# Decoder layer on one core: the loads, the out-projection and the late softmax around the change of phase, put in another order

## The chip, the cores and the metric

One core of a Trainium2 chip. The time is the device time of one execution in microseconds (us). The kernel before ran three times: 1143.99, 1139.13 and 1143.78 us, median 1143.78.

## The reference

x and a context are 16 sequences of 256 rows of 512 values (4096 rows), float32.

```python
x = layernorm(x + attn(x) @ Wo.T + bo)      # per row: 32x32 scores over heads, softmax, a difference of two halves, RMS norm
r = scan(r * decay + ctx * ctx)             # along each sequence
x = layernorm(x + x * r)
h = relu(x @ w1.T) ** 2                     # 2048 wide, w1 and w2 ternary by groups of 64
x = layernorm(x + rmsnorm(h) @ w2.T)
```

The attention here mixes the 16 heads of one row with each other; it is small and private to the row, and takes many small matmuls, with a softmax on VectorE. Each float32 operand of a large matmul is split into an upper and a lower part.

## The kernel before

The 4096 rows are eight superblocks of 512 (`NSB` 8, four tiles of 128 rows each, `TT` 4). Every engine has its own program in order, tied to the others by semaphores, and the order is written out by hand.

**Phase A** (`phase_a`, bodies 0 to 7): body i projects superblock i to q, k and v (`project`, 12 groups of 12 matmuls, line 615), does the scores of i-1 (`scores`, four chunks of 64 matmuls, line 632) with their softmax, and the mix with v of i-2 (`mix`, line 651). Beside it the weights of the feed-forward part are made ternary in `w_in`: loaded on the SP queue (line 473 and 469), taken by ScalarE (line 941), worked on by GpSimd, and written back.

**The transition** stands after `phase_a` in each engine's program: scores of superblock 7 (`LATE`), the four `mix` chunks of superblock 6, and what superblock 0 needs before its feed-forward: `out_project` (line 740, 48 matmuls), `add_projection` (line 1330), `scan` of the squared context (line 1363), `x1_norm`, `add_scan` (line 1372), `x2_norm`, and the transposes of the result (`x2_transpose` line 774, `x2_upper` line 996 on ScalarE, `x2_lower` line 1390 on VectorE). `mixed_turn` (line 1242) on VectorE empties a mix bank and lets the next `mix` start; `out_lower` (line 1325) makes the lower half of the operand that `out_project` reads. SP issues the loads one by one: `dbd`, `ot` (line 522), the second half of q (line 402), `woh`, `wol`, `bob`, `xb`, `cx` (lines 543 to 547), then weights.

**Phase B** (`phase_b`, bodies 0 to 7): body i is the feed-forward of superblock i in 16 steps j: `up` (line 788), `hidden` on ScalarE (lines 1005 to 1015), `hidden_lower` (line 1398) and `hidden_sum` (line 1409) on VectorE, `down` (line 804) three steps behind. In the same steps stand the last norm of i-1 (`hidden_rms` line 1421, `add_hidden` line 1430) and all the preparation of i+1. So `out_project(i + 1, t)` stands at j = 2 to 5, and from t = 1 on waits for `add_projection(i + 1, t - 1)`; `x2_transpose(i + 1, ...)` stands at the end of the body. GpSimd adds the bias to `xb` (`add_bias`, line 1595, four instructions a body); in `body_b(i)` it adds that of i+1 and before the change waits for nothing but the load of `xb`. Superblock 7's softmax is fitted into bodies 0 to 2 of phase B: `late_clean`, `late_shift` (line 1188 to 1192), the exponential on ScalarE (line 928) and `late_second` (line 1201 to 1217), at steps that the tables `LATE_CLEAN`, `LATE_SHIFT`, `LATE_EXP` and `LATE_SECOND` give; its RMS scale (`o_scale`, line 1567) is GpSimd's in body 4.

The memory of a region is reused: `xb`, `cx` and `x2n` lie where the halves of the transposed x lay in phase A.

Of the kernel before, what the change touches and what calls it, by code (L numbers as in the profile page):

```python
# [29 lines left out]
P = 128  # L30
# [44 lines left out]
def program(nc, x_in, xt_in, ctx_in, w_qkvo, bo, lq1, lq2, lk1, lk2, decay, fc_in, proj_in, out):  # L75
# [11 lines left out]
    with ExitStack() as stack:  # L87
# [95 lines left out]
        vo = sb("x", "vo", [P, HD, G], F32)  # L183
        xb = sb("x", "xb", [P, TT, D], F32)
        bob = sb("x", "bob", [P, D], F32)
        cx = sb("x", "cx", [P, KC, SB], F32)
        x2n = sb("x", "x2n", [P, TT, D], F32)
        x2h = sb("x", "x2h", [P, KC, SB], F32R)
        x2l = sb("x", "x2l", [P, KC, SB], F32R)
# [170 lines left out]
        LATE_CLEAN = {1: 1, 4: 2, 11: 3}  # L360
        LATE_SHIFT = {1: 1, 4: 2, 13: 3}
        LATE_EXP = {1: 0, 2: 1, 6: 2, 14: 3}
        LATE_SECOND = {1: (0, 2), 2: (1, 3)}
        LATE_MIX = {(2, 11): 0, (3, 1): 1, (3, 4): 2, (4, 1): 3}
# [14 lines left out]
        def _(sp):  # L379
# [81 lines left out]
            def x_load(i, par):  # L461
                hold((f_ps, at(i - 1, 12, 0)) if later(i - 1) else (xa_ld, 16))
                sp.dma_start(x_raw[:, par, :, :], xt_in[i]).then_inc(xa_ld, 16)

            def w_load(i, u):

                if u:
                    hold((wt_wr, at(i, 32, 16)))
                    sp.dma_start(w_in[:].rearrange("p (r d) -> p r d", d=D), proj_in[i]).then_inc(wt_ld, 16)
                    return  # L470
                if later(i):
                    hold((wt_wr, at(i, 32, 0)))
                sp.dma_start(w_in[:].rearrange("p (k n) -> p k n", k=KC), fc_in[i]).then_inc(wt_ld, 16)
# [23 lines left out]
            def body(i, par, do_2, do_1):  # L497
                if later(i) and not (isinstance(i, int) and i == NSB - 1):
                    x_load(i + 1, 1 - par)
# [24 lines left out]

            def cx_load(i):
                sp.dma_start(cx[:], ctx_in[i]).then_inc(cx_ld, 16)

            def w1_load(n):
# [12 lines left out]
            ot_load(0)  # L541
            second_half_load(NSB - 1)
            sp.dma_start(woh[:].bitcast(F32), wo_scr[0]).then_inc(wo_ld, 16)
            sp.dma_start(wol[:].bitcast(F32), wo_scr[1]).then_inc(wo_ld, 16)
            sp.dma_start(bob[:], bo.rearrange("(a n) -> a n", a=1).to_broadcast([P, D])).then_inc(bo_ld, 16)
            sp.dma_start(xb[:], x_t[0]).then_inc(xb_ld, 16)
            cx_load(0)

            w_write(NSB - 1, 1)
# [6 lines left out]
            w1_load(1)  # L556
            o_write(NSB - 2)
            w2_load(1)
            hold((rs_ps, TT))
            cx_load(1)  # L560
            hold((x2_done, TT))
            sp.dma_start(xb[:], x_t[1]).then_inc(xb_ld, 16)

            def body_b(i, prep, fin):
# [35 lines left out]
        def _(pe):  # L600
# [239 lines left out]
            mix(NSB - 2, 2, 0, G // 4)  # L840
            scores(NSB - 1, 2, 0, FULL)
            mix(NSB - 2, 3, 0, G // 4)
            for t in range(TT):
                out_project(0, t)
            scores(NSB - 1, 3, 0, FULL)
            for t in range(TT):
                scan_transpose(0, t)
            for t in range(TT):
                x2_transpose(0, t)
# [34 lines left out]
        def _(act):  # L884
# [141 lines left out]
            for t in range(1, LANES, 2):  # L1026
                act.dma_start(dbd[H * t:H * (t + 1), t, :, :],
                              dt[H * t:H * (t + 1), :, :]).then_inc(dbd_ld, 16)
            mixed(NSB - 2, 0)
            mixed(NSB - 2, 1)  # L1030
            out_upper(0)
            mixed(NSB - 2, 2)
            mixed(NSB - 2, 3)
            for k in range(KC):
                ctx_square(0, k)
            for t in range(TT):
                x2_upper(0, t)

            def body_b(i, prep, fin, ahead):
                for j in range(HC):  # L1040
# [15 lines left out]
                    if not later(i) and j == 0:  # L1056
                        out_upper(1)
                    if not later(i) and j in LATE_EXP:
                        exps(LATE, LATE_EXP[j])
                    if (i, j - 1) in LATE_MIX:  # L1060
# [23 lines left out]
        def _(v):  # L1084
# [356 lines left out]
            late_turn(0)  # L1441
            late_turn(1)
            mixed_turn(NSB - 2, 0)
            mixed_turn(NSB - 2, 1)
# [3 lines left out]
            out_lower(0)  # L1448
            late_turn(2)
            mixed_turn(NSB - 2, 3)  # L1450
            square_sum(NSB - 2, 2)
            square_sum(NSB - 2, 3)
            rms_seed(NSB - 2)
            add_projection(0, 0)
            add_projection(0, 1)
            v.wait_ge(dec_ld, 64)
            scan(0, range(2))
            add_projection(0, 2)
            scan(0, range(2, 4))
            add_projection(0, 3)  # L1460
            late_turn(3)
            x1_norm(0)
            for t in range(TT):
                add_scan(0, t)
            x2_norm(0)
            for t in range(TT):
                x2_lower(0, t)

            def body_b(i, prep, fin, ahead):
                if not later(i):  # L1470
                    late_clean(0)
                for c in LATE_SECOND.get(i, ()):
                    late_second(c)
                for j in range(HC):
# [33 lines left out]
                    if not later(i) and j in LATE_SHIFT:  # L1508
                        late_shift(LATE_SHIFT[j])
                    if (i, j) == (2, 0):  # L1510
                        late_diff_turn()
# [19 lines left out]
        def _(pool):  # L1531
# [70 lines left out]
            def body_b(i, prep, fin, ahead):  # L1602
                if prep:
                    for t in range(TT):
                        add_bias(i + 1, t)
# [49 lines left out]
```

## Time and profile before

| | |
|---|---|
| median of three executions | 1143.78 us |
| the profiled execution's own time | 1143.45 us |
| its span, first to last instruction | 1141.6 us |
| TensorE busy | 1047.9 us, 92% |
| VectorE, ScalarE, GpSimd busy | 928.6, 566.6, 245.2 us |
| mean granted TensorE clock | 0.963 |

The profile is of one execution; 1.85 us lie outside its span. In a row of the timeline the first number is the start in us from the span's start, the second the duration, and a bracket gives the idle time of that engine before the row and what ended it. PE is TensorE, DVE VectorE, ACT ScalarE, POOL GpSimd, SPq and ACTq are the DMA issues of SyncE and ScalarE. The granted clock is a share of 2.4 GHz; 0.50 is 1.2 GHz. Phase A ends near 451 us, the first `up` of body 0 starts at 519.5 us, and bodies 1 to 6 take 73.6 to 80.5 us each.

### The profile page before, as it was taken

What the parts mean: (1) busy time and instruction counts of PE and PEld (TensorE: products, weight loads), DVE (VectorE), ACT (ScalarE), POOL (GpSimd) and SP (SyncE); (2) the same over time, 40 slices, a digit from 0 to 9 for tenths busy, and PEclk for the clock granted to TensorE, in tenths of its full rate; (3) what the DMA queues carried; (4) which work ended last, traced back from release to release, by engine and by line L of the source; (5) the groups of instructions that cost most, each with busy time, mean ns of one, the idle gap of its engine ahead of it and who ended that gap; (6) DMA issues with size and microseconds to landing.
All of it is one profiled execution on the core that took longest, in us unless ns stands there. A gap on an engine that the chain in (4) does not pass through costs nothing.

```text
span 1141.6 us, 19562 instructions
## 1 busy us (share of the span) xinstructions
PE 1047.9 (92%) x7008; PEld 826.8 (72%) x7008; DVE 928.6 (81%) x1669; ACT 566.6 (50%) x866; POOL 245.2 (21%) x238
## 2 busy tenths in 40 slices
PE   7999999998999998727989999999999999999994
PEld 5777667676776766515867888878877788888883
DVE  4579898888888998596987998978969969798555
ACT  5442424243434342205556566665663766656672
POOL 6212433434252425131020020020023100200000
PEclk9999999999999999867998999999999999999997
DMA  7977686859596859892120223312202303110011
GB/s 277 306 183 177 144 238 129 247 133 240 134 246 137 213 144 210 239 358 83 38 74 1 74 75 61 112 44 50 106 1 74 111 2 88 61 38 1 1 37 37
DMA packets 167469, 140.50 MB, mean 123 GB/s; under 512 B 140368, under 2 KB 140880, under 8 KB 161488
## 3 DMA queue, kind: packets, MB, share of 16 engines
q1 hardware_dynamic: 96080, 113.83, 36.3%
q10 hardware_dynamic: 71296, 25.43, 9.1%
q8 instruction: 58, 0.95, 0.4%
q14 instruction: 35, 0.29, 0.1%
HBM read 82.61 MB, written 52.95 MB: 119 GB/s over the span
## 4 chain that ended last, share of the span: by engine, by line
PE 61%; DVE 17%; DMA 6%; ACT 6%; issue 5%; SPq 4%; ACTq 1%; DVEq 0%
PE ps_s L804 17%; PE ps_f L788 17%; PE ps_f L615 11%; PE ps_s L632 6%; PE ps_o L740 5%; SPq L432 2%; SPq L402 2%; DVE row_sum L1144 1%; DMA cx<-in_ctx_turned 1%; DMA w_in<-in_fc_turned 1%; DVE cx L1363 1%; DMA w_scr<-w_in 1%; DMA w_raw<-in_qkvo 1%; DMA qbd<-q_scr 1%; ACT f_sb L913 1%
## 5 line engine op out<-in xcount | busy, mean ns | idle before, releaser
L788 PE MATMUL ps_f<-x2h,w 128*128 128x512 f32 x512 | 205.4, 401 | 1.6 <-DVE x2l L1390 1.6
L788 PE MATMUL ps_f<-x2l,w 128*128 128x512 f32 x512 | 201.4, 393 | 0.0
L804 PE MATMUL ps_s<-w,hh 128*128 128x512 f32 x500 | 198.5, 397 | 2.8 <-DVE hl L1398 2.8
L804 PE MATMUL ps_s<-w,hl 128*128 128x512 f32 x500 | 196.5, 393 | 0.0
L615 PE MATMUL ps_f<-xth,wh 128*128 128x512 f32 x376 | 156.6, 416 | 3.4 <-issue 2.7
L1398 DVE TENSOR_TENSOR hl<-h_sb,hh 128x512 fp32r<-128x512 f32 x128 | 93.1, 727 | 81.7 <-ACT hh L1015 81.5
L615 PE MATMUL ps_f<-xtl,wh 128*128 128x512 f32 x376 | 147.8, 393 | 0.0
L615 PE MATMUL ps_f<-xth,wl 128*128 128x512 f32 x376 | 147.7, 393 | 0.0
L632 PE MATMUL ps_s<-qbd,k 128*32 128x128 f32 x2048 | 124.9, 411 | 15.3 <-DMA qbd<-q_scr 15.3
L1595 POOL TENSOR_TENSOR xb<-xb,bob 128x512 f32<-128x512 f32 x32 | 48.8, 1554 | 403.3 <-DMA xb<-in_x 403.3
L632 PEld LDWEIGHTS ps_s<-qbd,k 128*32 128x32 f32 x2048 | 83.0, 147 | 52.4 <-issue 12.8
L1005 ACT ACTIVATE r_sb<-ps_f 128x512 f32<-128x512 f32 x128 | 75.5, 590 | 87.3 <-PE ps_f L788 87.3
L1023 ACT ACTIVATE h_sq<-h_sb 128x512 f32<-128x512 f32 x128 | 79.4, 620 | 74.4 <-DVE h_acc L1409 74.4
L788 PEld LDWEIGHTS ps_f<-x2h,w 128*128 128x128 f32 x512 | 97.6, 191 | 22.2 <-issue 2.5
L788 PEld LDWEIGHTS ps_f<-x2l,w 128*128 128x128 f32 x512 | 97.5, 190 | 19.5
L804 PEld LDWEIGHTS ps_s<-w,hh 128*128 128x128 f32 x500 | 94.8, 190 | 22.6 <-issue 3.2
L804 PEld LDWEIGHTS ps_s<-w,hl 128*128 128x128 f32 x500 | 94.9, 190 | 19.3
L1576 POOL TENSOR_TENSOR w_in<-w_in,gscale 128x512 f32<-128x512 f32 x32 | 52.7, 1646 | 225.2 <-DVE gscale L1269 212.2
L615 PEld LDWEIGHTS ps_f<-xth,wh 128*128 128x128 f32 x376 | 71.7, 191 | 31.2 <-issue 15.5
L913 ACT ACTIVATE f_sb<-ps_f 128x512 f32<-128x512 f32 x64 | 38.4, 599 | 112.4 <-PE ps_f L615 108.9
L1409 DVE TENSOR_TENSOR h_acc<-h_acc,h_sq 128x512 f32<-128x512 f32 x112 | 84.2, 752 | 0.1
L1015 ACT ACTIVATE hh<-h_sb 128x512 fp32r<-128x512 f32 x128 | 81.0, 633 | 4.1
(160 smaller groups left out, 1830.7 us busy)
## 6 DMA issues: line engine op xcount, KB each, us to landing
q_scr<-f_sb ACTq DMA_DIRECT2D x32, 256.0 KB, 4.3
k_scr<-f_sb ACTq DMA_DIRECT2D x32, 256.0 KB, 2.7
w_scr<-w_in SPq DMA_DIRECT2D x16, 512.0 KB, 5.8
k<-k_scr SPq DMA_DIRECT2D x8, 1024.0 KB, 8.0
qbd<-q_scr SPq DMA_DIRECT2D x128, 64.0 KB, 4.7
v_scr<-f_sb ACTq DMA_DIRECT2D x32, 256.0 KB, 5.7
ot<-o_scr SPq DMA_DIRECT2D x32, 256.0 KB, 4.6
xb<-in_x SPq DMA_DIRECT2D x8, 1024.0 KB, 5.3
```

Of the source, the lines that this page charges most:

```text
L615: last = nc.tensor.matmul(ps_f[:, n % 2, :], w[:, n // 4, k, cols], xx[:, par, k, :], start=(k == 0 and xx is xth and w is wh), stop=(k == ...
L632: last = nc.tensor.matmul(ps_s[32 * j:32 * (j + 1), 2 * (c % 2) + gq // 4, (gq % 4) * P:(gq % 4 + 1) * P], k2[:, :, g], qbd[:, :, :, g].re ...
L740: last = nc.tensor.matmul(proj_bank(i, t), a[:, k, rows], w[:, k, :], start=(k == 0 and w is woh and a is oth), stop=(k == KC - 1 and a is ...
L788: last = nc.tensor.matmul(ps_f[:, j % 2, :], w1[:, j // 2, k, (j % 2) * P:(j % 2 + 1) * P], xx[:, k, :], start=(k == 0 and xx is x2h), sto ...
L804: last = nc.tensor.matmul(ps_s[:, t, :], a[:, j % 4, t * P:(t + 1) * P], w2[:, j, :], start=(j == 0 and a is hh), stop=(j == HC - 1 and a ...
L913: nc.scalar.activation(f_sb[:, n % 3, :], ps_f[:, n % 2, :], ACT.Copy).then_inc(f_ev, 1)
L1005: nc.scalar.activation(r_sb[:], ps_f[:, j % 2, :], ACT.Relu).then_inc(r_done, 1)
L1015: nc.scalar.activation(hh[:, j % 4, :], h_sb[:, j % 4, :], ACT.Copy).then_inc(hh_done, 1)
L1023: nc.scalar.activation(h_sq[:, j % 2, :], h_sb[:, j % 4, :], ACT.Square).then_inc(hq_done, 1)
L1398: nc.vector.tensor_tensor(hl[:, j % 4, :], h_sb[:, j % 4, :], hh[:, j % 4, :].bitcast(F32), ALU.subtract).then_inc(hl_done, 1)
L1409: nc.vector.tensor_tensor(h_acc[:], h_sq[:, 0, :] if j == 1 else h_acc[:], h_sq[:, j % 2, :], ALU.add).then_inc(ha_done, 1)
L1576: nc.gpsimd.tensor_tensor(w_in[:, half(r)], w_in[:, half(r)], gscale[:, half(r)], ALU.mult).then_inc(wt_md, 1)
```

## The change

- Memory: in region x, `x2n` and then `cx` and `x2h` now follow `xb`, and `bob` lies behind `x2h`. `xb` and `cx` so lie where nothing is read any more once body 6 of phase A has projected.
- SP: `cx` and `xb` of superblock 0 are issued at the start of body 7 of phase A, behind the projections of body 6. In the transition `woh` and `wol` go ahead of the second half of q of superblock 7, and `o_write(6)` goes behind the load of `xb` of superblock 1.
- TensorE: `out_project(0, ...)` stands before `scores(7, 2)` and `scores(7, 3)`; the latter stands behind the second `scan_transpose`.
- ScalarE: the context is squared before `mixed(6, 0)`.
- VectorE: the whole scan stands before `mixed_turn(6, 0)`, `late_turn(2)` behind `x1_norm(0)`, `late_turn(3)` behind `x2_norm(0)`.
- Late softmax: `late_shift(3)` goes from step 13 of body 0 to the start of body 1, its exponential from (0, 14) to (1, 0), `late_second(2)` from the start of body 1 to its step 6.
- GpSimd: `add_bias(i + 1, ...)` waits until the first `up` of body i is done.

```diff
-        LATE_SHIFT = {1: 1, 4: 2, 13: 3}
-        LATE_EXP = {1: 0, 2: 1, 6: 2, 14: 3}
-        LATE_SECOND = {1: (0, 2), 2: (1, 3)}
+        LATE_SHIFT = {1: 1, 4: 2}
+        LATE_EXP = {(0, 1): 0, (0, 2): 1, (0, 6): 2, (1, 0): 3}
+        LATE_SECOND = {1: (0,), 2: (1, 3)}
...
             def body(i, par, do_2, do_1):
-                if later(i) and not (isinstance(i, int) and i == NSB - 1):
+                if isinstance(i, int) and i == NSB - 1:
+                    hold((f_ps, at(i, 12, 0)))
+                    cx_load(0)
+                    sp.dma_start(xb[:], x_t[0]).then_inc(xb_ld, 16)
+                elif later(i):
                     x_load(i + 1, 1 - par)
...
             ot_load(0)
-            second_half_load(NSB - 1)
             sp.dma_start(woh[:].bitcast(F32), wo_scr[0]).then_inc(wo_ld, 16)
             sp.dma_start(wol[:].bitcast(F32), wo_scr[1]).then_inc(wo_ld, 16)
+            hold((f_wr[0], at(NSB, 64, 0)))
             sp.dma_start(bob[:], ...).then_inc(bo_ld, 16)
-            sp.dma_start(xb[:], x_t[0]).then_inc(xb_ld, 16)
-            cx_load(0)
-
+            second_half_load(NSB - 1)
...
-            o_write(NSB - 2)
             w2_load(1)
...
             sp.dma_start(xb[:], x_t[1]).then_inc(xb_ld, 16)
+            o_write(NSB - 2)
...
-            scores(NSB - 1, 2, 0, FULL)
             mix(NSB - 2, 3, 0, G // 4)
             for t in range(TT):
                 out_project(0, t)
-            scores(NSB - 1, 3, 0, FULL)
+            scores(NSB - 1, 2, 0, FULL)
             for t in range(TT):
                 scan_transpose(0, t)
+                if t == 1:
+                    scores(NSB - 1, 3, 0, FULL)
...
             late_turn(1)
+            v.wait_ge(dec_ld, 64)
+            scan(0, range(KC))
             mixed_turn(NSB - 2, 0)
...
             out_lower(0)
-            late_turn(2)
             mixed_turn(NSB - 2, 3)
...
-            late_turn(3)
             x1_norm(0)
+            late_turn(2)
             for t in range(TT):
                 add_scan(0, t)
             x2_norm(0)
+            late_turn(3)
...
+                if i == 1:
+                    late_shift(3)
...
+                    if (i, j) == (1, 6):
+                        late_second(2)
...
                 if prep:
+                    pool.wait_ge(f1_ps, at(i, HC, 1))
                     for t in range(TT):
                         add_bias(i + 1, t)
```

## Rows read from the trace of the kernel before

**Rows 1.** The page's busy times, all engines' first row.

```profile
PE 1047.9 (92%) x7008; PEld 826.8 (72%) x7008; DVE 928.6 (81%) x1669; ACT 566.6 (50%) x866; POOL 245.2 (21%) x238
```

**Rows 2.** Windows: stretch, length, busy of PE, PEld, DVE, ACT, POOL, clock, DMA.

```profile
601.30:610.50 9.20, 9.15 (x33) 7.61 (x34) 5.39 (x9) 3.47 (x7) 0.00 (x0) 0.70 0.01 2
...
919.50:993.10 73.60, 73.60 (x346) 61.04 (x345) 61.94 (x145) 47.20 (x78) 6.43 (x4) 1.00 0.20 58
```

**Rows 3.** Chain of waits, 400 to 620 us: start, duration, what.

```profile
469.08 13.71 DMA cx<-in_ctx_turned
```

**Rows 4.** Timeline of SP and of ACT in bodies 6 and 7 of phase A.

```profile
340.91 6.09 SPq L432 DMA_DIRECT2D dbd<-dt  x8
...
398.85 5.16 SPq L432 DMA_DIRECT2D dbd<-dt  x8
...
411.60 1.06 ACT L941 ACTIVATE w_b<-w_in 128x1024 bf16<-128x1024 f32 x1 [3.00 <-DMA w_in<-in_fc_turned]
```

**Rows 5.** Page, DMA issues: engine, count, size, us from issue to landing.

```profile
xb<-in_x SPq DMA_DIRECT2D x8, 1024.0 KB, 5.3
```

**Rows 6.** Timeline of DVE in the transition.

```profile
459.97 1.04 DVE L1242 STREAM_TRANSPOSE o_sb<-ps_o 128x512 f32<-128x512 f32 x1
...
466.95 2.29 DVE L1325 TENSOR_TENSOR otl<-ot,oth 128x2048 fp32r<-128x2048 f32 x1
...
489.29 2.62 DVE L1363 TENSOR_TENSOR_SCAN cx<-dec,cx 128x256 f32<-128x256 f32 x4
...
501.28 0.69 DVE L1372 SCALAR_TENSOR_TENSOR xb<-ps_t,xb 128x512 f32<-128x512 f32 x1
...
508.54 0.17 DVE L1345 BATCH_NORM_AGGREGATE moments<-stats 128x2 f32<-128x6 f32 x1
```

**Rows 7.** Timeline of PE: first out-projection, the scores behind it, first `up` of superblock 0.

```profile
474.83 0.47 PE L740 MATMUL ps_f<-woh,oth 128*128 128x512 f32 x1 [0.51 <-DMA wol<-wo_scr]
...
485.91 3.92 PE L632 MATMUL ps_s<-qbd,k 128*32 128x128 f32 x64
...
519.49 0.77 PE L788 MATMUL ps_f<-x2h,w 128*128 128x512 f32 x1 [1.57 <-DVE x2l L1390]
```

**Rows 8.** Timeline of the four engines at the end of body 0.

```profile
591.72 1.78 DVE L1398 TENSOR_TENSOR hl<-h_sb,hh 128x512 fp32r<-128x512 f32 x1
...
598.87 1.06 ACT L928 ACTIVATE late<-late 128x1024 f32<-128x1024 f32 x1 [6.79 <-DVE late L1192]
...
590.68 6.86 POOL L1595 TENSOR_TENSOR xb<-xb,bob 128x512 f32<-128x512 f32 x4 [63.59 <-DMA xb<-in_x]
...
601.35 1.08 PE L774 MATMUL ps_t<-ident,x2n 128*128 128x128 f32 x4 [6.42 <-DVE x2l L1390]
```

**Rows 9.** Timeline of PE, later short waits: body 2's start, bodies 2 and 3's ends.

```profile
697.43 0.50 PE L740 MATMUL ps_o<-woh,oth 128*128 128x512 f32 x1 [0.48 <-DVE xb L1330]
...
755.18 0.63 PE L774 MATMUL ps_t<-ident,x2n 128*128 128x128 f32 x4 [1.62 <-DVE x2l L1390]
...
832.45 0.63 PE L774 MATMUL ps_t<-ident,x2n 128*128 128x128 f32 x4 [0.51 <-DVE x2l L1390]
```

**Rows 10.** Timeline of POOL and DVE where GpSimd scales in body 4.

```profile
877.73 5.04 POOL L1567 TENSOR_TENSOR vo<-vo,o_rs 128x512 f32<-128x512 f32 x4
...
880.33 1.21 DVE L290 TENSOR_TENSOR nt<-ln_rs 128x4 f32<-128x4 f32 x1
```

**Rows 11.** Timeline of DVE and PE at the start of body 5.

```profile
923.49 0.69 DVE L1398 TENSOR_TENSOR hl<-h_sb,hh 128x512 fp32r<-128x512 f32 x1 [5.17 <-ACT hh L1015]
...
930.97 0.68 DVE L1330 TENSOR_TENSOR xb<-ps_o,xb 128x512 f32<-128x512 f32 x1
...
932.11 0.39 PE L740 MATMUL ps_o<-woh,oth 128*128 128x512 f32 x1
```

**Rows 12.** PE's wait in body 4 (timeline), and the window around it.

```profile
885.89 0.47 PE L804 MATMUL ps_s<-w,hh 128*128 128x512 f32 x1 [2.80 <-DVE hl L1398]
...
880.00:890.00 10.00, 7.20 (x30) 0.84 0.01 2
```

More of the change, by code:

```diff
@@ L184, in program @@
         xb = sb("x", "xb", [P, TT, D], F32)
+        x2n = sb("x", "x2n", [P, TT, D], F32)
+        cx = sb("x", "cx", [P, KC, SB], F32)
+        x2h = sb("x", "x2h", [P, KC, SB], F32R)
         bob = sb("x", "bob", [P, D], F32)
-        cx = sb("x", "cx", [P, KC, SB], F32)
-        x2n = sb("x", "x2n", [P, TT, D], F32)
-        x2h = sb("x", "x2h", [P, KC, SB], F32R)
         x2l = sb("x", "x2l", [P, KC, SB], F32R)
@@ L463, in x_load, with cx_load @@
                 sp.dma_start(x_raw[:, par, :, :], xt_in[i]).then_inc(xa_ld, 16)
+            def cx_load(i):
+                sp.dma_start(cx[:], ctx_in[i]).then_inc(cx_ld, 16)
             def w_load(i, u):
@@ L523, in ot_load @@
                                  o_scr[i, :, c * P:(c + 1) * P, :].rearrange("t p g -> p t g")).then_inc(ot_ld, 16)
-            def cx_load(i):
-                sp.dma_start(cx[:], ctx_in[i]).then_inc(cx_ld, 16)
             def w1_load(n):
@@ L1028, in _ @@
                               dt[H * t:H * (t + 1), :, :]).then_inc(dbd_ld, 16)
+            for k in range(KC):
+                ctx_square(0, k)
             mixed(NSB - 2, 0)
@@ L1033, in _ @@
             mixed(NSB - 2, 3)
-            for k in range(KC):
-                ctx_square(0, k)
             for t in range(TT):
@@ L1057, in body_b @@
                         out_upper(1)
-                    if not later(i) and j in LATE_EXP:
-                        exps(LATE, LATE_EXP[j])
+                    if (i, j) in LATE_EXP:
+                        exps(LATE, LATE_EXP[i, j])
                     if (i, j - 1) in LATE_MIX:
@@ L1453, in _ @@
             rms_seed(NSB - 2)
[L1454 to L1460, printed above, removed]
-            late_turn(3)
+            for t in range(TT):
+                add_projection(0, t)
             x1_norm(0)
+            late_turn(2)
             for t in range(TT):
```

## Prediction

> **What bounds the kernel now.** I read the page's busy times, then windows body by body, then the chain of waits, then each engine's timeline where TensorE pauses. TensorE is busy 92% of the span [rows 1]. Body 5 of phase B runs 73.6 us without a gap at full clock [rows 2]: there only a pause of TensorE costs or gives time. The pauses that this change touches are two. In the transition the chain runs through the load of `cx`, 13.7 us, then squares, scans, two norms and transposes on VectorE, ending at the `x2l` that the first `up` waits for [rows 3, 7]. At the end of body 0 TensorE waits 6.42 us [rows 8].
>
> **Body 7 of phase A: two loads more.** `cx` and `xb`, 1 MB each, are issued about 7 us before the `dbd` loads, which wait for VectorE's transpose anyway. The wait ahead of them costs nothing: VectorE's covers it. But behind them on SP stand `dbd`, then `w_in`, and ScalarE already waits 3.00 us for `w_in` with projections queued behind [rows 4]. Body 6 had one 1 MB load in this place, and its eight `dbd` issues took 6.09 us against 5.16 [rows 4]. I take that, **+0.9 us**. Bounds: 0 (two loads landed in the 7 us) and, if both pass in full first, 2 x 5.3 - 7 = 3.6 [rows 5].
>
> **Transition.** The order on VectorE is now: turns of superblock 7, scan, then the mixed turns. The scan is two of the 2.62 us groups, 5.2 us, and pushes the first mixed turn from 459.97 to 465.2. From there to the end of `out_lower` (469.24) the members are the same: 9.3 us, so 474.5 [rows 6]. The out-projection started at 474.83, held by `wol` [rows 7]; `wol` now lands earlier, but `otl` is the late one. So it starts no earlier. Its 48 matmuls took 11.1 us, to the scores at 485.91; TensorE has done only four short mixes in the 14 us before, so I add one loss of clock, 1.6 us (10 us at 0.84 [rows 12]): 487.3. Add and statistics of the last tile 1.4, first norm 4.7 (508.54 to 513.2 [rows 6]) plus 1 for a collision with GpSimd, `late_turn(2)` 1.25, four scan additions 7.2 (501.28 to 508.5), second norm 4.7, and 6.3 from its end to the first `up` (513.2 to 519.49): 513.9. **-5.6 us.** Bounds: -8.3 (neither clock nor collision), 0 (another order of wait, such as `scores(7, 2)` on the way to the transposes, takes it all). `scores(7, 2)` and `(7, 3)`, 3.9 us each, lie beside the norm. `late_turn(3)` (1.25) lies beside the transposes. `o_write(6)` leaves the queue ahead of weights; 7 MB from about 496 still land `cx` of superblock 1 by about its use, so 0; without that cover ScalarE would wait for it in step 0.
>
> **End of body 0.** GpSimd's four bias additions, 590.7 to 597.5, stretch `hl` from 0.69 to 1.78 us; then `late_shift(3)` runs; its exponential blocks ScalarE for 6.79 us, and with it `x2_upper`, `x2_lower` and TensorE's transpose [rows 8]. All of this leaves. What is late next is `hl` of step 14, at about 593.6, then `x2l` at 594.8, when TensorE is just free. So the whole 6.4 us go. Behind the pause stand 9.2 us at a clock of 0.70 [rows 2], 0.30 x 9.2 = 2.7 us. **-9.1 us** (bounds -9.1 and -5, if the shift meets the same engines in body 1). The smaller waits at the ends of bodies 2 and 3, 1.62 and 0.51 us, are from the same additions [rows 9]: **-2.1 us**.
>
> **Starts of bodies 1 to 6: the additions come back.** They are not removed; they now run from the end of the first `up`. Where GpSimd works beside small VectorE steps, each of its instructions of 1.26 us (5.04 / 4) makes one VectorE instruction wait: 1.21 us instead of 0.16, +1.05 [rows 10]. In body 5 `up` ends near 921.3, so the additions would run 921.4 to 927.5. `hl` starts at 923.49, the eleven steps of `hidden_rms` follow, and the first `add_projection` ends at 931.65; TensorE wants it at 932.11 [rows 11]. There is 0.46 us of slack and no idle time on the way but 0.2. The additions cost VectorE 0.4 (rest of the second) + 2 x 1.05 = 2.5 us, TensorE 2.5 - 0.46 = 2.1. That holds for bodies 5 and 6 (4.2). In 3 and 4 a late mix, 1.1 us of TensorE, gives it more to do first, so the slack is near 1.2: 1.3 each (2.6). In 2, two `late_second` stand in front and VectorE meets all four additions: 4.2 less 0.5 of idle, 3.7, on top of the 0.48 already waited [rows 9]. In 1, 4.2 less 1.4 of idle, slack and lighter work, 2.8, plus 1.3 because `late_second(2)`, 3.1 us, now stands ahead of the scan additions that feed two transposes: 4.1. **Sum +14.6 us.** Bounds: 0 (the adds find gaps, as in the ends of bodies 1, 4 and 5, where TensorE lost nothing) and six times 4.2 less slack, about +21.
>
> The page "SBUF — State Buffer" of the Trainium skill (section "Who interferes with whom") says that a VectorE instruction with two SBUF inputs and a GpSimd instruction that reads SBUF exclude each other for the whole of the one that started. The trace agrees in kind: 1.05 of 1.26 us. By the full 1.26 the term would be about 2 us more.
>
> **Clock at those starts.** A pause of 2.80 us brought a loss of 1.6 us [rows 12]; one of 1.62 us brought none I can see [rows 9]. Of the six, the pause of body 2 (4.2) is long enough: **+1.6 us**. Bounds 0 and six times 1.6.
>
> **The sum.** 0.9 - 5.6 - 9.1 - 2.1 + 14.6 + 1.6 = +0.3. On the profiled execution's 1143.45 us (0.3 below the median of the runs) that gives 1143.8; I say 1144. About 0.5%, 5.7 us, is what a measurement can tell from no change. This forecast, gains and returned cost within that of each other: 0.42.
>
> **Rivals.**
> - *The start of a body absorbs the additions* (0.35). For it: in the ends of bodies 1, 4 and 5 they overlap VectorE and TensorE never waits, and their order against `hl` is a matter of tenths. Against it: the slack of 0.46 us and VectorE's unbroken row of work [rows 11]. With none of the cost, 0.9 - 5.6 - 9.1 - 2.1 = -15.9: 1127.6. With half of it, 1135. It decides from where the starts and their clock cost under 10 us together.
> - *Each pause at a start costs the clock too* (0.16), slower. The place is the second `out_project` of bodies 1 to 6. If pauses of 2.1 us are long enough, five more losses of 1.6 us: +8, 1152. It decides from four more losses on. For it: 2.80 us was enough; against: 1.62 was not.
> - *The loads in body 7 hold up the SP queue* (0.07). Two such loads at 5.3 us each [rows 5] need 10.6 us and have 7; `dbd` and `w_in` land up to 3.6 us later and phase A ends so much later: 1147, or above 1150 together with the previous one.
> - The change doing nothing is excluded for the end of body 0: the instructions named there are moved. In the transition it can be so, since the scan now stands before the out-projection: then 1149.4, inside the range.
>
> **The numbers.** Likeliest 1144 us. The range reaches to the absorbing case with nearly none of the cost, 1129, and to the clock case with a few us of SP delay, 1155. Faster by over 0.5%: 0.35. Within: 0.42. Slower: 0.23 (the clock, and the SP delay or the bounds of the starts on top).
>
> **What would show it.** Right: the first `up` at about 514 to 515; no wait before line 774 in body 0 and full clock behind it; GpSimd's line 1595 right behind each first `up`, `hidden_rms` steps of 1.2 us beside it, and TensorE waiting some 2 us for `xb` (line 1330) before line 740 in bodies 1 to 6. Wrong: no such waits (then faster), clock below 1.00 in their windows (then slower), or ScalarE waiting over 4 us for `w_in` in body 7 of phase A.

## The result and the profile after

| | before | changed |
|---|---|---|
| median of nine executions | 1140.32 us (1137.57 to 1143.99) | 1146.32 us (1143.23 to 1149.23) |
| ratio | | 1.0046, 95% interval 1.003 to 1.0063 |
| span of the profiled execution | 1141.6 us | 1145.1 us |

The change makes the kernel slower, clear of noise: by 0.46% or 5.2 us by the ratio, which goes by the means, and by 6.0 us between the medians. The half per cent, 5.7 us, that the prediction called no change lies between these two numbers and inside the interval. Of the page, the rows that answer to [rows 1]:

```profile
PE 1051.8 (92%) x7008; PEld 826.7 (72%) x7008; DVE 929.8 (81%) x1669; ACT 565.9 (49%) x866; POOL 243.1 (21%) x238
```

VectorE, ScalarE and GpSimd are as busy as before to within 2.1 us. TensorE does the same 7008 matmuls and is busy 3.9 us longer, in a span that is 3.5 us longer: its pauses have the same sum, 93.3 us against 93.7. So the change moved the pauses, and TensorE then worked longer between them; where, and at which clock, is what the rest has to show. The timeline of PE, with the rows where it waited from the first `up` on, answers to [rows 7] and [rows 9] (the lines have moved: 790 was 788, 742 was 740, 776 was 774):

```profile
513.87 0.77 PE L790 MATMUL ps_f<-x2h,w 128*128 128x512 f32 x1 [1.57 <-DVE x2l L1393]
525.64 0.77 PE L742 MATMUL ps_o<-woh,oth 128*128 128x512 f32 x1 [4.25 <-issue]
536.27 0.50 PE L742 MATMUL ps_o<-woh,oth 128*128 128x512 f32 x1 [1.31 <-DVE xb L1333]
612.49 0.50 PE L742 MATMUL ps_o<-woh,oth 128*128 128x512 f32 x1 [2.06 <-DVE xb L1333]
646.29 0.66 PE L762 MATMUL ps_t<-ident,cx 128*128 128x128 f32 x4 [0.98 <-DVE xb L1375]
693.20 0.80 PE L742 MATMUL ps_o<-woh,oth 128*128 128x512 f32 x1 [3.89 <-DVE xb L1333]
773.42 0.50 PE L742 MATMUL ps_o<-woh,oth 128*128 128x512 f32 x1 [0.51 <-DVE xb L1333]
...
933.49 0.50 PE L742 MATMUL ps_o<-woh,oth 128*128 128x512 f32 x1 [1.60 <-DVE xb L1333]
1009.01 0.50 PE L742 MATMUL ps_o<-woh,oth 128*128 128x512 f32 x1 [1.59 <-DVE xb L1333]
```

The first `up` is 5.6 us earlier on the axis of the profile, of which 4.2 belong to the transition (table below), and no pause before line 776 is left: the 6.42 us of [rows 8] and the two of [rows 9] are gone. In their place TensorE waits in each of bodies 1 to 6 for the first `add_projection` (line 1333). Why is seen in the timelines of POOL and DVE at the start of body 5, which answer to [rows 11]:

```profile
921.05 5.49 POOL L1599 TENSOR_TENSOR xb<-xb,bob 128x512 f32<-128x512 f32 x4 [38.71 <-PE ps_f L790]
```

```profile
923.11 1.03 DVE L1401 TENSOR_TENSOR hl<-h_sb,hh 128x512 fp32r<-128x512 f32 x1 [5.51 <-ACT hh L1018]
924.06 0.15 DVE L1424 TENSOR_SCALAR h_ms<-ps_t 128x4 f32<-128x4 f32 x1
924.25 1.07 DVE L288 TENSOR_SCALAR h_rs<-h_ms 128x4 int32<-128x4 int32 x1
925.36 1.21 DVE L290 TENSOR_TENSOR nt<-h_rs 128x4 f32<-128x4 f32 x1
926.60 0.16 DVE L291 SCALAR_TENSOR_TENSOR nt<-nt,h_ms 128x4 f32<-128x4 f32 x1
```

GpSimd now starts on the end of `up` and ends at 926.54. Three VectorE instructions in that time take 1.03, 1.07 and 1.21 us, where they take 0.69, 0.17 and 0.16 without GpSimd beside them: 2.3 us more together. The next is as short as ever, once GpSimd is done. The one that reads PSUM (line 1424) is not touched.

The windows of the changed kernel show where the clock fell, for [rows 2] and [rows 12]. The granted clock is the third figure from the end of a row, ahead of the DMA share and the GB/s; the first row has all engines, the others PE alone:

```profile
470.00:480.00 10.00, 7.33 (x45) 5.63 (x46) 7.06 (x8) 3.50 (x3) 6.91 (x7) 0.50 0.80 231
...
610.00:620.00 10.00, 7.94 (x28) 0.83 0.00 0
690.00:700.00 10.00, 6.80 (x19) 0.66 0.84 111
880.00:890.00 10.00, 7.17 (x29) 0.83 0.01 2
```

**The table by stretches.** The mean square (line 833, 831 before) comes once a body, right behind its first `up`, and cuts phase B well. In the changed kernel bodies 1 and 2 lie between these rows:

```profile
599.35 0.95 PE L833 MATMUL ps_t<-ones,h_acc 128*128 128x1 f32 x8
678.22 0.94 PE L833 MATMUL ps_t<-ones,h_acc 128*128 128x1 f32 x8
759.85 0.95 PE L833 MATMUL ps_t<-ones,h_acc 128*128 128x1 f32 x8
```

Ahead of them I cut at the `o_scr<-o_sb` issue before body 7 of phase A, at the transpose of superblock 6's differences (`dt<-p`), and at the first `up`. All rows of the table are differences of such starts, in us; "body 0" goes from the first `up` to the first mean square. The columns behind "changed" are experiments, told below; "best" is the one with the shortest time.

| stretch | before | changed | wait alone | softmax alone | transition alone | changed, no wait | staged | best |
|---|---|---|---|---|---|---|---|---|
| start, to that issue | 391.5 | 388.5 | 390.3 | 387.1 | 392.2 | 392.9 | 389.9 | 390.8 |
| body 7 of A, to `dt` | 61.0 | 62.6 | 60.3 | 60.4 | 63.4 | 62.7 | 61.6 | 60.8 |
| transition, to first `up` | 67.0 | 62.8 | 66.7 | 66.9 | 62.2 | 61.2 | 60.6 | 58.4 |
| body 0 | 92.7 | 85.5 | 89.0 | 89.6 | 94.1 | 93.6 | 83.5 | 83.7 |
| body 1 | 73.7 | 78.9 | 78.3 | 77.4 | 73.7 | 77.3 | 78.9 | 76.4 |
| body 2 | 77.6 | 81.6 | 80.5 | 77.6 | 76.5 | 77.6 | 76.6 | 76.6 |
| body 3 | 77.3 | 78.3 | 78.2 | 77.3 | 77.3 | 77.3 | 76.6 | 76.6 |
| body 4 | 80.5 | 82.7 | 82.5 | 80.5 | 80.0 | 80.5 | 80.9 | 80.8 |
| bodies 5, 6 each | 73.6 | 75.5 | 75.5 | 73.6 | 73.6 | 73.6 | 73.8 | 73.8 |

The first row is scatter: up to there all kernels do the same, and it spans 387.1 to 392.9. Between before and changed it is TensorE's clock: idle 26.2 and 26.3 us, busy 365.2 and 362.2 at a mean granted clock of 0.98 and 1.00. So the two profiles differ by 3.5 us, though the changed one had begun body 7 2.9 us early; without that it is 6.4, near the 6.0 of the medians. The rows below add up to it: +1.6 - 4.2 - 7.2 + 5.2 + 4.1 + 1.0 + 2.2 + 1.9 + 1.9 = +6.5 by the rounded numbers.

The same stretches, from the start of body 7 on, divide these 6.4 us between waiting and working. TensorE is idle for 67.5 us before and 67.0 in the changed kernel, and busy for 682.7 and 689.6. These are the windows of the transition, body 0, body 1 and body 2, before and then changed:

```profile
452.50:519.49 66.99, 37.52 (x441) 0.73 0.91 296
519.49:612.15 92.66, 82.15 (x344) 0.92 0.13 36
612.15:685.86 73.71, 73.71 (x346) 1.00 0.20 58
685.86:763.42 77.56, 75.46 (x378) 1.00 0.34 79
```

```profile
451.12:513.87 62.75, 41.08 (x453) 0.74 0.78 231
513.87:599.35 85.48, 79.86 (x345) 0.94 0.24 77
599.35:678.22 78.87, 75.83 (x345) 0.98 0.19 54
678.22:759.85 81.63, 77.74 (x378) 0.96 0.32 75
```

Body 7 and the transition together work 3.3 us longer, body 0 works 2.3 shorter, body 1 2.1 longer and body 2 2.3 longer. The pauses that went and those that came have the same sum; what the change costs is longer work, most of it in stretches where the clock fell.

### The profile page after: what moved, and what is told of

It is laid out like the page before. It is cut to its first block, busy times and chain, and to the rows that moved or that the text cites. A ratio compares the mean times of both kernels' runs of the same rounds, so it can differ in the third digit from the quotient of the medians.

```text
span 1145.1 us, 19569 instructions
## 1 busy us (share of the span) xinstructions
PE 1051.8 (92%) x7008; PEld 826.7 (72%) x7008; DVE 929.8 (81%) x1669; ACT 565.9 (49%) x866; POOL 243.1 (21%) x238
## 4 chain that ended last, share of the span: by engine, by line
PE 48%; DVE 27%; ACT 7%; issue 6%; DMA 6%; SPq 4%; ACTq 1%; DVEq 0%
PE ps_s L806 16%; PE ps_f L790 14%; PE ps_f L617 5%; PE ps_s L634 4%; PE ps_o L742 4%; SPq L432 3%; DMA w_in<-in_fc_turned 2%; DVE row_sum L1147 2%; DMA w_scr<-w_in 2%; DVE cx L1366 2%; DVE hl L1401 2%; DVE res L1433 1%; DVE nt L290 1%; DMA qbd<-q_scr 1%; DVE xtl L1097 1%
## 5 line engine op out<-in xcount | busy, mean ns | idle before, releaser
L1401 DVE TENSOR_TENSOR hl<-h_sb,hh 128x512 fp32r<-128x512 f32 x128 | 90.9, 710 | 82.7 <-ACT hh L1018 82.4
L790 PEld LDWEIGHTS ps_f<-x2h,w 128*128 128x128 f32 x512 | 97.4, 190 | 22.2 <-issue 2.5
L806 PEld LDWEIGHTS ps_s<-w,hh 128*128 128x128 f32 x500 | 94.1, 188 | 22.4 <-issue 3.2
L1014 ACT ACTIVATE h_sb<-r_sb 128x512 f32<-128x512 f32 x128 | 80.9, 632 | 4.1
```

The source lines that it names most:

```text
L790: last = nc.tensor.matmul(ps_f[:, j % 2, :], w1[:, j // 2, k, (j % 2) * P:(j % 2 + 1) * P], xx[:, k, :], start=(k == 0 and xx is x2h), sto ...
L806: last = nc.tensor.matmul(ps_s[:, t, :], a[:, j % 4, t * P:(t + 1) * P], w2[:, j, :], start=(j == 0 and a is hh), stop=(j == HC - 1 and a ...
L1014: nc.scalar.activation(h_sb[:, j % 4, :], r_sb[:], ACT.Square).then_inc(h_done, 1)
L1401: nc.vector.tensor_tensor(hl[:, j % 4, :], h_sb[:, j % 4, :], hh[:, j % 4, :].bitcast(F32), ALU.subtract).then_inc(hl_done, 1)
```

## The experiments

Every ratio is against runs of the kernel before on the same chip. Each experiment has one profile.

**The wait alone.** The kernel before with GpSimd's new wait, and the changed kernel without it.

```diff
 def body_b(i, prep, fin, ahead):       # GpSimd, on the kernel before
     if prep:
+        pool.wait_ge(f1_ps, at(i, HC, 1))
         for t in range(TT):
             add_bias(i + 1, t)
```

> The kernel before with nothing but GpSimd's new wait. Theory 1: bodies 1 to 6 start 1.5 to 4 us later each (about +15 net of the short waits at the ends of bodies 2 and 3), and the wait at the end of body 0 shrinks from 6.4 to about 3 us because hidden_lower is not slowed but the exponential still blocks ScalarE: about 1151 us. Theory 2: about as before, 1140. Theory 3: the end of body 0 loses its whole wait, 9 us, and the sum is 1146 or less.

Measured 1152.06 us, ratio 1.0097 (1.0079 to 1.0116), as theory 1 had it. The waits stand where they do in the changed kernel:

```profile
596.45 0.84 PE L774 MATMUL ps_t<-ident,x2n 128*128 128x128 f32 x4 [3.23 <-DVE x2l L1390]
620.07 0.50 PE L740 MATMUL ps_o<-woh,oth 128*128 128x512 f32 x1 [2.71 <-DVE xb L1330]
699.58 0.79 PE L740 MATMUL ps_o<-woh,oth 128*128 128x512 f32 x1 [3.89 <-DVE xb L1330]
...
938.48 0.50 PE L740 MATMUL ps_o<-woh,oth 128*128 128x512 f32 x1 [1.60 <-DVE xb L1330]
```

The pause at the end of body 0 goes from 6.42 to 3.23 us, half, since the softmax still blocks ScalarE. Bodies 1 to 6 pay 14.3 us, body 0 gives 3.7.

```diff
 def body_b(i, prep, fin, ahead):       # GpSimd, in the changed kernel
     if prep:
-        pool.wait_ge(f1_ps, at(i, HC, 1))
         for t in range(TT):
```

> The changed kernel without GpSimd's new wait (the bias additions run again as soon as xb is there). Theory 1, the returned cost lies in the additions beside the starts of bodies: bodies 1 to 6 lose the 1 to 4 us each that they gained (body 1 keeps about 1.3 us), TensorE waits some 2 us at the end of body 0 again because GpSimd slows hidden_lower there; about 1133 us, 13 below the changed kernel and 7 below the one before. Theory 2, the late softmax in bodies 1 and 2 is what makes them longer: little changes, 1142 to 1147. Theory 3, the wait is what freed the end of body 0: its 9 us come back and nearly all of the gain at the starts is given back, 1140 or more.

Measured 1141.45 us, ratio 0.9993 (0.9979 to 1.0006). This is a miss for theory 1, which said 1133. Bodies 2 to 6 do return to their old lengths, as it said. But body 0 is at 93.6 us, not 87, and body 1 at 77.3, not 75. Theory 3 had the half of it that I had not: inside the changed kernel the wait frees most of the end of body 0. Theory 2 was right for body 1 alone. The next one separates them.

**The softmax alone.** The tables `LATE_SHIFT`, `LATE_EXP` and `LATE_SECOND` of the change and their calls, on the kernel before.

```diff
-        LATE_SHIFT = {1: 1, 4: 2, 13: 3}
-        LATE_EXP = {1: 0, 2: 1, 6: 2, 14: 3}
-        LATE_SECOND = {1: (0, 2), 2: (1, 3)}
+        LATE_SHIFT = {1: 1, 4: 2}
+        LATE_EXP = {(0, 1): 0, (0, 2): 1, (0, 6): 2, (1, 0): 3}
+        LATE_SECOND = {1: (0,), 2: (1, 3)}
...
+                if i == 1:
+                    late_shift(3)
...
+                    if (i, j) == (1, 6):
+                        late_second(2)
```

> The kernel before with nothing but the late softmax moved (the shift, the exponential and one second half of superblock 7). Theory 1: TensorE's wait at the end of body 0 falls from 6.4 us to about 2, without a loss of clock, body 1 gains 1 to 1.5: about 1134 us. Theory 2, that the softmax lengthens bodies 1 and 2: 1141 to 1145.

Measured 1142.67 us, ratio 1.0007 (0.9994 to 1.002): no gain, and a miss for theory 1, which said 1134. Its timelines of DVE and POOL at the end of body 0:

```profile
586.52 1.79 DVE L1398 TENSOR_TENSOR hl<-h_sb,hh 128x512 fp32r<-128x512 f32 x1
588.23 1.77 DVE L1409 TENSOR_TENSOR h_acc<-h_acc,h_sq 128x512 f32<-128x512 f32 x1
589.93 1.75 DVE L1398 TENSOR_TENSOR hl<-h_sb,hh 128x512 fp32r<-128x512 f32 x1
591.60 1.75 DVE L1409 TENSOR_TENSOR h_acc<-h_acc,h_sq 128x512 f32<-128x512 f32 x1
593.27 0.68 DVE L1390 TENSOR_TENSOR x2l<-ps_t,x2h 128x512 fp32r<-128x512 f32 x1
```

```profile
585.22 7.58 POOL L1599 TENSOR_TENSOR xb<-xb,bob 128x512 f32<-128x512 f32 x4 [64.18 <-DMA xb<-in_x]
```

With the shift out of the way, all four additions fall on instructions with two operands in SBUF, which lose 4.3 us together, and TensorE waits 4.37 us. Before, `late_shift`'s reduction took one of them without harm (1.21 us, as in the kernel with the wait alone, where GpSimd is idle there). So of the 9.0 us that the changed kernel saves from the second out-projection of body 0 on, neither part gives the whole: in the same stretch the wait alone gives 4.2, the softmax alone 3.1. And body 1 pays 3.6 us for it, in three pauses (0.38, 1.55 and 1.03 us), where I had found one.

**The transition alone.** The changed kernel with softmax tables and GpSimd's wait as before.

```diff
-        LATE_SHIFT = {1: 1, 4: 2}
-        LATE_EXP = {(0, 1): 0, (0, 2): 1, (0, 6): 2, (1, 0): 3}
-        LATE_SECOND = {1: (0,), 2: (1, 3)}
+        LATE_SHIFT = {1: 1, 4: 2, 13: 3}
+        LATE_EXP = {1: 0, 2: 1, 6: 2, 14: 3}
+        LATE_SECOND = {1: (0, 2), 2: (1, 3)}
...
-                    pool.wait_ge(f1_ps, at(i, HC, 1))
```

> The kernel before with nothing but the memory, the order of loads and the order of the transition changed. The profiles so far give, from the transpose of superblock 6's differences to the first up of body 0, 67.0 us before and 60.6 to 62.8 with the new order, and 1.2 to 2.0 us more in body 7 of phase A. Additive theory: this alone gives -5 + 1.5 = -3.5 us, against which the start of body 0 loses 1 to 2 us because xb of superblock 1 lands later: 1139 to 1140 against 1141.6 before; body 1 stays at 73.7 us. Rival, the moved scan only pays together with the moved softmax: the first up comes as late as before and the time is 1142 or more.

Measured 1140.17 us, ratio 0.9976 (0.9957 to 0.9995): the additive theory, -2.7 us. The transition gives 4.8, body 7 takes 2.4, body 0 1.5, and bodies 2 and 4 are 1.1 and 0.5 shorter. In body 2 TensorE waits 0.51 us at the end where it waited 1.62 (1.65 to 1.69 in two other kernels with the additions in their old place); why is not shown.

So the parts alone are +11.1, +0.8 and -2.7 us, +9.2 together, against +5.3 for the whole (0.46%). The 3.9 us between them are about what the four intervals allow together, so the medians do not show that the parts work together. The stretches show where they do not add. In body 0 the whole saves 7.2 us and the parts 5.3, since its end needs both the wait and the softmax. In body 1 the whole costs 5.2 and the parts 8.3: its pauses are 2.7 us with the wait alone, 3.0 with the softmax alone and 3.0 with both. Bodies 2 and 4, body 7 and the transition take 4.5 us of this back, so that over all stretches the parts come within 0.5 us of the whole.

**Staged additions.** Whether the additions must cost anything is asked by giving them another place: the first of a body behind the first `up`, before `hidden_lower` comes; three behind the first `add_projection`, where VectorE waits for ScalarE.

```diff
                     pool.wait_ge(f1_ps, at(i, HC, 1))
                     for t in range(TT):
+                        if t == 1:
+                            pool.wait_ge(y_done, at(i + 1, TT, 1))
                         add_bias(i + 1, t)
```

> The changed kernel, with the first of a body's four additions behind the first up and the other three behind the first add_projection. Theory 1: the first addition is done before hidden_lower comes, the others fall where VectorE waits for ScalarE; the starts cost nearly nothing and the ends stay free: about 1130 us, second out-projections without a wait except in body 2 (0.5 us), body 5 at 73.6 us. Theory 2: bodies 1 and 2 stay at 79 and 81 us, 1140. Rival to the staging: the three additions slow the next add_projection, which TensorE wants 6.6 us after the first, and the wait moves to the third out-projection: 1138.

Measured 1132.99 us, ratio 0.9923 (0.9906 to 0.9941), where theory 1 said about 1130. Bodies 5 and 6 are at 73.8 us without a wait of TensorE; body 2 waits 0.97 us at its second out-projection, 0.5 was expected; the steps at the start of body 5 are short again, and the collision has moved to where nobody waits (POOL, then DVE):

```profile
908.65 1.28 POOL L1599 TENSOR_TENSOR xb<-xb,bob 128x512 f32<-128x512 f32 x1 [38.70 <-PE ps_f L790]
918.96 4.25 POOL L1599 TENSOR_TENSOR xb<-xb,bob 128x512 f32<-128x512 f32 x3 [9.02 <-DVE xb L1333]
```

```profile
910.72 0.69 DVE L1401 TENSOR_TENSOR hl<-h_sb,hh 128x512 fp32r<-128x512 f32 x1 [5.54 <-ACT hh L1018]
...
921.98 1.77 DVE L1412 TENSOR_TENSOR h_acc<-h_acc,h_sq 128x512 f32<-128x512 f32 x1
```

The rival to the staging falls. Body 1 stays at 78.9: that is the softmax, as theory 2 said of this one body (with the old tables, in the next experiment, it is 74.2).

The same on the kernel before, which has no wait of its own there:

```diff
 def body_b(i, prep, fin, ahead):       # GpSimd, on the kernel before
     if prep:
+        pool.wait_ge(f1_ps, at(i, HC, 1))
         for t in range(TT):
+            if t == 1:
+                pool.wait_ge(y_done, at(i + 1, TT, 1))
             add_bias(i + 1, t)
```

> The kernel before with nothing but the staged additions (the first behind the first up, three behind the first add_projection). The wait alone, all four behind the first up, cost 1.0%. Theory 1: the place of the additions is all that counts; bodies 1 to 6 are as long as before or 0.5 to 1.5 us shorter (2 and 3), the stretch with body 0 loses 3.7 us as with the wait alone: ratio 0.995 to 0.996. Rival, any wait on GpSimd's in-order program costs the next add_projection: ratio 1.000 or above.

Measured 1136.77 us, ratio 0.9958 (0.9945 to 0.9971). The same wait that costs 1.0% with four additions behind it gains 0.4% with one: the place is all that counts.

**The softmax's place.** Two variants of the staged kernel: `late_second(2)` back at the start of body 1; and, beside that, `late_shift(3)` back at step 13 of body 0 with its exponential left at (1, 0).

```diff
-        LATE_SECOND = {1: (0,), 2: (1, 3)}
+        LATE_SECOND = {1: (0, 2), 2: (1, 3)}
...
-                    if (i, j) == (1, 6):
-                        late_second(2)
```

> The staged kernel with the late second half of chunk 2 back at the start of body 1 (the shift still there too). Body 1 is now 78.9 us against 73.7, with waits of 0.38 us before the second out-projection and 2.24 before the third scan transpose. If the step at j = 6 makes the second of them, that one goes and the first grows to 2 to 3.5 us, because 3.1 us more stand ahead of hidden_lower: body 1 at 77 to 79, the whole within 2 us of the staged kernel, 1133. If the second wait has another cause, both stand and body 1 is 81.

Measured 1131.44 us, ratio 0.9908 (0.9886 to 0.9931). The 2.24 us before the scan transpose are gone, and the second out-projection waits 2.09 in place of 0.38. Body 1 is 76.5 us, 2.4 less than staged: the pauses are 2.1 us in sum against 2.6, and the staged kernel had also lost clock (0.50 from 642 to 644 us). Over all profiles of staged kernels body 1 is 76.4, 76.5, 76.5 and 77.7 us with this half at the start of body 1, and 78.9 and 77.3 with it at step 6: the sign is likely, the size open, and the intervals of the two ratios overlap.

```diff
-        LATE_SHIFT = {1: 1, 4: 2}
+        LATE_SHIFT = {1: 1, 4: 2, 13: 3}
...
-                if i == 1:
-                    late_shift(3)
```

> The staged kernel with the shift of chunk 3 back at step 13 of body 0 (its exponential stays at the start of body 1) and both second halves at the start of body 1. ScalarE is then not blocked at the end of body 0; the 2.7 us of the shift can hold hidden_lower of step 14 and the transposes: a wait of 0 to 2.7 us there. Body 1 returns to 73.7 to 74.5. Expected 1129 to 1130, 3 us under the staged kernel. Rival: the exponential in body 1 is what lengthens it, and it stays at 77 or more.

Measured 1134.88 us, ratio 0.9936 (0.9913 to 0.996); 1129 to 1130 was expected. Body 1 is 74.8, as hoped, but body 0 is 90.7 against 83.5. Of these 7.2 us the shift accounts for some 4.4: it holds the transposes for 2.67 us even without GpSimd beside it, and the clock is 0.50 from 592 to 594 us behind that. The rest is a loss of clock at the start of the body (0.50 from 530 to 536 us, behind a pause of 2.93 us), which the shift does not touch. So the half of the change that takes the shift out of body 0 is right, by less than 7.2 us.

**The scan in the gaps.** On the staged kernel:

```diff
             v.wait_ge(dec_ld, 64)
-            scan(0, range(KC))
             mixed_turn(NSB - 2, 0)
+            scan(0, range(0, 1))
             mixed_turn(NSB - 2, 1)
             square_sum(NSB - 2, 0)
+            scan(0, range(1, 2))
             mixed_turn(NSB - 2, 2)
...
             mixed_turn(NSB - 2, 3)
+            scan(0, range(2, KC))
```

> The staged kernel with the scan no longer in one piece ahead of the mixed turns: one quarter behind the first turn, one behind the second, the half behind the fourth, where VectorE waits for mixes and the out-projection. If the scan's 4.7 us ahead of the mixed turns are what holds the out-projection, it starts 3 to 4.5 us earlier and the whole is 3 to 4 us faster than the staged kernel, 1129. If the loads of wo or the operand of ScalarE hold it, nothing changes.

Measured 1129.38 us, ratio 0.9895 (0.9872 to 0.9918), 3 us better than staged, though the two intervals overlap. The transition is 58.2 us against 60.6. In the changed kernel, the scan and the first mixed turn are these:

```profile
458.95 4.73 DVE L1366 TENSOR_TENSOR_SCAN cx<-dec,cx 128x256 f32<-128x256 f32 x8
463.59 1.01 DVE L1245 STREAM_TRANSPOSE o_sb<-ps_o 128x512 f32<-128x512 f32 x1
...
471.41 3.10 DVE L1328 TENSOR_TENSOR otl<-ot,oth 128x2048 fp32r<-128x2048 f32 x1
```

and here a quarter of the scan takes the place of an idle 1.2 us between two turns, and `otl` is ready at 467.05:

```profile
457.77 1.04 DVE L1245 STREAM_TRANSPOSE o_sb<-ps_o 128x512 f32<-128x512 f32 x1 [0.40 <-PE ps_o L653]
458.67 1.21 DVE L1366 TENSOR_TENSOR_SCAN cx<-dec,cx 128x256 f32<-128x256 f32 x2
460.11 1.04 DVE L1245 STREAM_TRANSPOSE o_sb<-ps_o 128x512 f32<-128x512 f32 x1 [0.24 <-PE ps_o L653]
...
464.76 2.29 DVE L1328 TENSOR_TENSOR otl<-ot,oth 128x2048 fp32r<-128x2048 f32 x1 [0.18 <-ACT oth L982]
```

Counted from the transpose of the differences, the out-projection starts 3.8 us earlier than in the staged kernel, now held by the load of `wol` (PE):

```profile
468.45 0.77 PE L742 MATMUL ps_f<-woh,oth 128*128 128x512 f32 x1 [2.36 <-DMA wol<-wo_scr]
```

Some 1.7 us of this are lost again in the first norm, where GpSimd now meets two small instructions: the collision that the prediction had put there (DVE):

```profile
483.06 0.82 DVE L1350 TENSOR_SCALAR ln_x<-moments 128x4 f32<-128x4 f32 x1
483.91 1.24 DVE L288 TENSOR_SCALAR ln_rs<-ln_x 128x4 int32<-128x4 int32 x1
```

That the gaps are the cause of the shorter time is not shown. With the scan in one piece the same transition takes 62.8, 62.2, 61.2 and 60.6 us in four profiles, but 58.8 and 57.9 in the two kernels of the paragraph before, whose code is the same there; with the scan in the gaps it takes 58.2 to 58.7 in four. In those two the scan began 4.8 us behind the transpose instead of 6.9 to 7.8, since VectorE did not have to wait for the scores ahead of it. The gaps make the stretch steady; against these two they gain nothing.

**The last three.** Staged, gaps and `late_second(2)` at the start of body 1 together; the same with the two early loads behind the q load of body 7; the first of them with `xb` of superblock 1 ahead of the second half of `w2`.

```diff
                 if do_1:
                     second_half_load(i - 1)
+                if isinstance(i, int) and i == NSB - 1:      # taken from ahead of dbd_load
+                    hold((f_ps, at(i, 12, 0)))
+                    cx_load(0)
+                    sp.dma_start(xb[:], x_t[0]).then_inc(xb_ld, 16)
```

> Staged additions, scan in the gaps of the mixed turns, and the late second half of chunk 2 at the start of body 1. If the parts add: the staged kernel 8.7 us under before, the gaps another 3.6, the second half between 0 and 1.5: ratio 0.988 to 0.989, 1128 to 1129 at a before of 1141.8. Body 1 at 76.5 us, from the transpose of superblock 6's differences to the first up 58 us. If the gaps and the clock work against each other the ratio stays at 0.990 or above.

Measured 1130.53 us, ratio 0.9899 (0.9875 to 0.9923): no better than the gaps without the second half. The transition is 58.3 us as expected. Against the kernel with that half at the same place and the scan in one piece (0.9908), the gaps are worth 0.1% here, which is nothing that can be told from noise.

> The same, with cx and xb of superblock 0 issued in body 7 of phase A behind the q load instead of ahead of dbd. If these two loads are what lengthens body 7 (61.0 us from o_write to the transpose of the differences before, 62.6 in the changed kernel), it returns to 60.3 to 61.1 and the time falls by 1 to 1.5 us. If body 7's length is scatter between executions, nothing changes.

Measured 1126.77 us, ratio 0.9874 (0.9848 to 0.99), the shortest time of all, 3.8 us under the one before it by the medians and 3.2 by the means, where 1 to 1.5 was expected; its interval overlaps those of its neighbours. Body 7 is 60.8 us against 64.1 in the one before, which is among the longest. Over all profiles it is 60.3 to 61.0 where no load stands ahead of `dbd` (five of them) and 61.3 to 64.1 where two do (nine): a cost of about 2 us, and not scatter.

```diff
             w1_load(1)
-            w2_load(1)
             hold((rs_ps, TT))
             cx_load(1)
             hold((x2_done, TT))
             sp.dma_start(xb[:], x_t[1]).then_inc(xb_ld, 16)
+            w2_load(1)
```

> The first of these kernels with xb of superblock 1 loaded ahead of the second half of w2. In the changed kernel the additions of body 0 began 7.0 us behind the first up (2.1 before) because xb landed late, met out_lower (3.0 us instead of 2.3), and from the first up to the second out-projection 22.4 us passed against 20.6. If that is the cause, the addition starts 3 us after the first up or earlier, and 20.6 us or less pass; the whole gains 0 to 1.5 us. If it is the clock that differs there, the 20 to 22 us scatter as before.

Measured 1130.03 us, ratio 0.9899 (0.9871 to 0.9926): nothing. The addition comes 3.8 us after the first `up` in place of 6.4, and 20.6 us pass to the second out-projection, where all staged kernels have 20.2 to 20.6, also those whose one addition comes at 7.0. The kernels with four additions in a row at 6.8 to 7.0 us have 22.2 to 22.4, the wait alone with four at 3.8 us has 21.1, and four at 1.7 or 2.1 us have 20.6. So it takes both, a late start and a row of four: in the changed kernel `out_lower` loses 0.7 us to them and the small instruction of the late softmax behind it 1.1 (line 1193, 1.25 us for 0.18), and staging had mended it already.

## Why the prediction was right

The forecast was a sum of +0.3 us, called no change, at 1144 us with 1129 to 1155. Measured are +5.2 us by the means (0.46%) and 1146.3 us. The mechanism is the one foretold: the pauses went where it said and came back where it said. That the forecast of no change holds is partly luck, for the cost came out just under the half per cent. And the 1144 is near to 1146.3 only because the base was high: it was 1143.45, and the kernel before has a median of 1140.32 over nine executions. The errors of the terms all go one way, 6.2 us together.

What was mis-sized is, most of all, the clock. Counted as TensorE's waiting, the terms make 0.9 - 7.2 - 6.4 + 12.5 = -0.2 us, and measured are -0.5. Counted as work at the lower clock, they make 1.6 - 2.7 + 1.6 = +0.5, and measured are +6.9 of longer work, all but 1.5 of it outside bodies 3 to 6, where the clock hardly changed. Two of the prediction's own signs of a slower result were there: a clock below 1.00 at the starts of bodies 1 and 2 (0.83 and 0.66), and ScalarE waiting over 4 us for `w_in`. Term by term, as the prediction put them:

- **Body 7 of phase A, +0.9.** It was +1.6 here and about 2 over all profiles. The row it was read from had one load; two were added. The eight `dbd` issues took 5.84 us for 5.16, which is 0.7; most of the rest is the `w_scr` write behind them, whose landing `w_in` waits for (4.0 us from issue to issue, before 3.2). ScalarE's wait for `w_in` rose as said, from the 3.00 of [rows 4] to 4.74:

```profile
410.36 1.06 ACT L944 ACTIVATE w_b<-w_in 128x1024 bf16<-128x1024 f32 x1 [4.74 <-DMA w_in<-in_fc_turned]
```

- **Transition, -5.6.** It was -4.2. That the first `up` stood at 513.87 us, where the prediction had 513.9, is luck: the profile had begun body 7 2.9 us early and lost 1.6 in it. The chain is the one that was named: scan (4.7), mixed turns, `otl`, out-projection. The collision in the norm did not come. Two things were missed: the last three mixes ran at the lower clock (1.94 us each, before 1.11, 1.94 and 1.47; the clock was 0.50 from 470 to 480), and `otl` took 3.10 us for 2.29, since `bob` now lands early and the additions of superblock 0 meet it. The size is that of one profile: the same order gave -4.2 to -9.1 over six of them.
- **End of body 0, -9.1.** It was -9.0: from the second out-projection to the mean square 63.1 us against 72.1. But it took the wait and the softmax together, and neither gives it alone; the prediction had them as one cause.
- **Start of body 0, not priced.** +1.8: the term that was missing. `xb` landed 7 us after the first `up`, and the additions met `out_lower` (3.02 us) and the late softmax behind it.
- **Ends of bodies 2 and 3, -2.1.** The pauses are gone.
- **Starts of bodies 1 to 6 with clock, +14.6 and +1.6.** The table gives +16.3 net of the -2.1, so 18.4 in place of 16.2. By bodies, the prediction's pauses were 2.8 and 1.3 in body 1 (measured 2.06 and 0.98), 4.2 in body 2 (3.89), 1.3 in 3 and 4 (0.51 in 3, 0.54 and 0.55 in 4, with 0.3 more at the late mix in each), 2.1 in 5 and 6 (1.60 and 1.59). All were a little shorter than said, and the bodies grew by more: in 5 and 6 by 1.9 with a pause of 1.6, in 1 and 2 by the clock, which fell in both, where it was counted once.

The rivals: that the starts absorb the additions is refuted by the wait alone (1.0097). The clock after each pause: it fell after the pauses of 2.06 and 3.89 us and not after those of 1.6, so the rival is true of two bodies out of six. The SP queue was late by 2 us, not by the 3.6 of the rival. The rule that the prediction took from "SBUF — State Buffer" of the Trainium skill (section "Who interferes with whom") held in kind in the rows of this case: a `TENSOR_TENSOR` with two operands in SBUF collides, one with an operand from PSUM does not, a reduction does not. A `TENSOR_SCALAR` with one operand in SBUF collided too (line 288, 1.07 us for 0.17), which the sentence in the prediction leaves out. A full collision costs 1.0 to 1.1 us, less than the 1.26 us of the GpSimd instruction, and less where that one is already under way (0.3 for `hl`). By the full 1.26 the sum of the prediction would have been 3.4 us more, with its sixteen full collisions, and not 2.

## What to carry to other kernels

A wait that moves GpSimd's work away from a collision moves the collision: look for the first VectorE instruction that TensorE waits for behind the new place, and put each addition where VectorE is idle, one at a time if need be. A part of a change that gains nothing alone (the softmax) can still be needed beside another, so the changes are to be tried together and apart. Add up what TensorE waits and what it works, each by itself: here the first did not change and the second cost 6.9 us. Work that is pulled ahead of a chain, as the scan was, can be put into the gaps of that chain instead; here it made the stretch steady, and a gain in time is not shown. Before a stretch is laid to a cause, compare it over all kernels that have the same code there.

## What was not expected

- A full collision costs VectorE the same, whatever its own length: 0.16 us became 1.21, 0.69 became 1.78. A string of eleven steps of 0.16 us lost as little as two long instructions, one collision for each GpSimd instruction.
- Bodies 5 and 6 repeat to within 0.1 us from kernel to kernel (73.6 in the four with the additions in their old place, 73.8 in the staged ones), while the stretch ahead of body 7, the same in all kernels, spreads over 5.8 us and the transition, with the same code, over 4.9. A profile's span compares badly at this size; its bodies compare well, as long as no pause near 2 us lies in them.
- The same 2.24 us pause gave a body 1 of 78.9 us in one profile and 77.3 in the other (staged, and with the scan in the gaps): the clock fell to 0.50 behind the first and stayed at 1.00 behind the second. Of five pauses of 2.06 to 2.09 us in body 1 the clock fell behind two.
